# A four-stage graph network kernel: 31 picked passes for 27, last-edge marks through the destination one-hots, one sum per pick, two transfers moved to ScalarE's queue

## What is computed

```
L0:  a_e   = tanh(relu(sum((x[src] @ A1' + b1) * (x[dst] @ A2' + b2 + rel_emb[type])) / sqrt(32)))
     nei   = segment_sum(a_e * sum_b w_comp[type, b] * (x[src] @ weight[b]), dst)
     curr  = x[src of the last edge of each node] @ self_loop_weight
     x     = norm(x + relu(nei + curr))
L1:  x     = norm(x + segment_sum(x[src], dst))
L2:  x     = norm(x + attention over the same edges)
L3:  x     = norm(x + ten propagation steps over the same edges)
```

## Time and profile before

| | us |
|---|---|
| median of 3 runs (lowest, highest) | 1147.88 (1146.41, 1151.34) |
| the profiled execution | 1148.57 |
| its span, first to last instruction | 1146.8 |
| busy: PE, DVE, ACT, POOL | 883.4, 933.5, 504.8, 608.6 |
| mean granted TensorE clock | 0.878 of 2.4 GHz |
| first product of the sweep (L1387) | 70.45 |
| last base columns (L1411) begin | 806.10 |

### The profile page before, as it was taken

How to read it: one execution, slowest core, us unless ns; L and a number is a source line. 1 busy time by engine, 2 the same in 40 slices (tenths; PEclk the granted TensorE clock), 3 DMA queues, 4 the chain that set the end, 5 groups by cost and what they waited for, 6 DMA issues and landing times.

```text
span 1146.8 us, 56069 instructions
## 1 busy us (share of the span) xinstructions
PE 883.4 (77%) x23682; PEld 838.9 (73%) x23682; DVE 933.5 (81%) x2369; ACT 504.8 (44%) x1244; POOL 608.6 (53%) x580
## 2 busy tenths in 40 slices
PE   2358887978686868777867768688468958999996
PEld 2357877877686867776767667587467958999996
DVE  8869999998898989898888988798557995555556
ACT  1135555554454546566756566556567400000000
POOL 5777777777777777777777777774000000000000
PEclk9569999888888888888988897978578979999998
DMA  4432333332232333232323322320000000000001
GB/s 117 60 75 55 64 59 60 66 57 51 48 60 54 57 52 59 52 57 57 57 56 56 51 54 50 68 45 13 5 2 3 4 2 4 5 4 4 4 5 19
DMA packets 54917, 47.97 MB, mean 42 GB/s; under 512 B 35966, under 2 KB 45182, under 8 KB 54662
## 3 DMA queue, kind: packets, MB, share of 16 engines
q0 software_dynamic: 18176, 9.34, 10.3%
q1 hardware_dynamic: 30822, 14.16, 6.1%
q10 hardware_dynamic: 5664, 20.84, 4.9%
HBM read 41.98 MB, written 2.31 MB: 39 GB/s over the span
## 4 chain that ended last, share of the span: by engine, by line
POOL 42%; DVE 19%; PE 18%; issue 16%; DMA 2%; ACT 2%; DVEq 0%; SPq 0%; ACTq 0%
POOL arena L631 42%; PE ps L883 14%; DVE arena L1372 2%; DVE arena L1612 2%; PE ps L854 2%; PE ps L893 2%; DVE arena L1411 2%; DVE arena L1632 1%; ACT arena L1120 1%; DMA arena<-line_table 1%; DMA arena<-rel_rows_in 1%; DVE aggT L1424 1%; DVE arena L1362 1%; PE ps L816 1%; DVE arena L1387 0%
## 5 line engine op out<-in xcount | busy, mean ns | idle before, releaser
L631 POOL DMA_INDIRECT arena<-x_pad,arena x568 | 606.8, 1068 | 173.4 <-issue 172.5
L816 PE MATMUL ps<-aggT 128*128 128x128 f16 x3024 | 217.3, 238 | 1.6 <-DVE aggT L1424 1.3
L816 PEld LDWEIGHTS ps<-aggT 128*128 128x128 f16 x3024 | 205.6, 110 | 3.1 <-DVE aggT L1424 3.1
L1372 DVE TENSOR_SCALAR arena<-pair_no,arena 128x275 bf16<-128x275 f16 (+2 forms) x784 | 183.1, 292 | 0.0
L883 PE MATMUL ps<-arena,adj_words 128*128 128x64 f16 x5625 | 171.9, 192 | 3.4 <-DVEq L1697 3.2
L883 PEld LDWEIGHTS ps<-arena,adj_words 128*128 128x128 fp8e4 x5625 | 170.5, 97 | 4.7 <-DVEq L1697 3.6
L1411 DVE TENSOR_TENSOR arena<-ps,arena 128x1536 f32<-128x1536 f32 x98 | 171.6, 1751 | 0.6
L1073 ACT ACTIVATE adj_words<-arena 128x500 uint8 x196 | 126.5, 646 | 56.5 <-ACT arena L1048 54.2
L1043 ACT ACTIVATE arena<-ps 128x500 fp8e4<-128x500 f32 x196 | 113.0, 577 | 86.9 <-PE ps L765 86.7
L758 PE MATMUL ps<-arena 128*128 128x25 bf16 x195 | 36.5, 187 | 148.7 <-DVE arena L1372 148.3
L778 PE MATMUL ps<-arena 128*32 128x44 f32 (+4 forms) x7048 | 131.3, 212 | 17.6 <-DVE arena L1411 17.5
(11 more groups left out here) (221 smaller groups left out, 1160.6 us busy)
## 6 DMA issues: line engine op xcount, KB each, us to landing
arena<-line_table ACTq DMA_DIRECT2D x48, 344.0 KB
arena<-x_pad,arena POOLq DMA_INDIRECT x568
arena<-pick_table SPq DMA_DIRECT2D x27, 256.0 KB
arena<-line_table ACTq DMA_DIRECT2D x48, 80.0 KB
arena<-dst_parts SPq DMA_DIRECT2D x196, 5.7 KB
agg_table<-arena SPq DMA_DIRECT2D x196, 2.5 KB
dst_parts<-aggT SPq DMA_DIRECT2D x1, 735.0 KB, 12.7
x<-x_pad SPq DMA_DIRECT2D x1, 400.0 KB
```

Of the source, the lines that this page charges most:

```text
L631: pool.indirect_dma_start(to, None, table, bass.IndirectOffsetOnAxis(ap=index, axis=0)).then_inc(done, 16)
L816: mm = nc.tensor.matmul(ps[:, at:at + PICK_WIDE * FEAT], pick_hot[:, u % PICK_RING, k * P:(k + 1) * P], x_parts[:, t, j * PICK_WIDE:(j + 1 ...
L1372: last = v.tensor_scalar(pair_hot[:, d % 2, k, 0:n], pair_no[:, 0:n], pair_of[:, d * DUO + k // SLOTS, k % SLOTS:k % SLOTS + 1], None, ALU ...
```

## The change

- `PICK_UNITS` becomes (3, 2, 2) alone: a duo is picked every three duos (5, 8, 11 to 95), 31 in all.
- The two adds of a pick become one reduction over the four candidates (L1441, L1445), which lie 32 values (128 bytes) apart.
- The one-hots of the destinations are made in pairs: the first of a pair is the last-edge mark, from `off_twice` = (offset + 1) x is-last, the second the destination, from offset + 1. Both are bf16. `weight_e` has pairs too: 1.0 and the weight. The weighting multiplies them and writes both into `mixed`, as its 17th and a new 18th column; the base columns are made from the 18th. The separate marks (L1397) go.
- ScalarE applies a relu after the tanh, with a wait between, since the weighting no longer clips.
- x is loaded by ScalarE's queue under a semaphore of its own, `x_loaded`; the second, larger store of the parts is issued by ScalarE's queue ahead of its first line loads.

```diff
--- before.py
+++ after.py
@@ -72,20 +72,20 @@
...
 PICK_LIMIT = 500.0
-PICK_UNITS = ((2, 2, 2, 1), (3, 2, 2))
+PICK_UNITS = ((3, 2, 2),)
...
     starts, units, picked, at = [], {}, [], 1
-    while at + len(PICK_UNITS[len(picked) % 2]) + 1 < DUOS:
+    while at + len(PICK_UNITS[len(picked) % len(PICK_UNITS)]) + 1 < DUOS:
         c, deep = len(picked), 0
-        for d, n in enumerate(PICK_UNITS[c % 2]):
+        for d, n in enumerate(PICK_UNITS[c % len(PICK_UNITS)]):
...
         starts.append(at)
-        at += len(PICK_UNITS[c % 2])
+        at += len(PICK_UNITS[c % len(PICK_UNITS)])
@@ -242,7 +242,7 @@
...
         hot_no = sb("hot_no", [P, HOTS], BF16)
-        next_no = sb("next_no", [P, HOTS], BF16)
+        next_no = sb("next_no", [P, HOTS, 2], BF16)
@@ -268,12 +268,13 @@
...
-        ARENA = 23880
+        ARENA = 23840
...
         base_t = stay.cut(GROUPS + 1, I32)
-        pair_of, dst_off, last_off_1 = [stay.cut(GROUPS * SLOTS).rearrange("p (g k) -> p g k", k=SLOTS) for _ in range(3)]
+        pair_of = stay.cut(GROUPS * SLOTS).rearrange("p (g k) -> p g k", k=SLOTS)
+        off_twice = stay.cut(2 * GROUPS * SLOTS, BF16).rearrange("p (g k i) -> p g k i", k=SLOTS, i=2)
@@ -293,6 +294,7 @@
...
         dst_t, next_t = [of.bitcast(I32).rearrange("p (g k) -> p g k", k=SLOTS) for of in (dst_words, next_words)]
+        dst_off, last_off_1 = [prep.cut(GROUPS * SLOTS).rearrange("p (g k) -> p g k", k=SLOTS) for _ in range(2)]
@@ -311,13 +313,13 @@
...
         lines = sweep.cut(LINE_BUFS * LINE * WINDOW, BF16, n=SIDE).rearrange("p (h e) -> p h e", h=LINE_BUFS)
-        score, weight_e = [sweep.cut(2 * WIDE).rearrange("p (h k) -> p h k", h=2) for _ in range(2)]
-        dst_hot = sweep.cut(2 * LINE * SLOTS * HOTS, BF16).rearrange("p (h k d) -> p h k d", h=2, d=HOTS)
-        weighted = sweep.cut(WIDE * HOTS).rearrange("p (k d) -> p k d", k=WIDE)
+        score = sweep.cut(2 * WIDE).rearrange("p (h k) -> p h k", h=2)
+        weight_e = sweep.cut(2 * WIDE * 2).rearrange("p (h k i) -> p h k i", h=2, i=2)
+        dst_hot = sweep.cut(2 * LINE * SLOTS * HOTS * 2, BF16).rearrange("p (h k d i) -> p h k d i", h=2, d=HOTS, i=2)
...
         row_hot = sweep.cut(2 * WIDE * P, BF16).rearrange("p (h k v) -> p h k v", h=2, k=WIDE)
-        mixed = sweep.cut(2 * WIDE * HOTS * MIXES).rearrange("p (h k d m) -> p h k d m", h=2, k=WIDE, d=HOTS)
+        mixed = sweep.cut(2 * WIDE * HOTS * (MIXES + 1)).rearrange("p (h k d m) -> p h k d m", h=2, k=WIDE, d=HOTS)
@@ -402,7 +404,7 @@
...
-        inputs_loaded = sem("inputs_loaded")
+        inputs_loaded, x_loaded = sem("inputs_loaded"), sem("x_loaded")
@@ -420,7 +422,7 @@
...
         side_in = [sem(f"side_in_{u}") for u in range(SIDES)]
-        side_made = sem("side_made")
+        tanh_made = sem("tanh_made")
@@ -469,7 +471,7 @@
...
-        LOADS = 14
+        LOADS = 13
@@ -505,7 +507,7 @@
...
                 sp.dma_start(to, of).then_inc(edges_loaded, 16)
-            loads = [(x[:], x_pad.rearrange("(b p) f -> p b f", p=P)), (a12[:, 0:FEAT], a1_t), (a12[:, FEAT:2 * FEAT], a2_t),
+            loads = [(a12[:, 0:FEAT], a1_t), (a12[:, FEAT:2 * FEAT], a2_t),
@@ -530,7 +532,6 @@
...
             sp.dma_start(by_block[:, 0:FIRST_STORED], q_parts[:, 0:FIRST_STORED]).then_inc(first_parts_stored, 16)
-            sp.dma_start(by_block[:, FIRST_STORED:BLOCKS], q_parts[:, FIRST_STORED:BLOCKS]).then_inc(parts_stored, 16)
@@ -702,13 +703,14 @@
...
         def _(pe):
-            pe.wait_ge(inputs_loaded, 16 * LOADS)
+            pe.wait_ge(x_loaded, 16)
...
+            pe.wait_ge(inputs_loaded, 16 * LOADS)
@@ -1013,7 +1015,9 @@
...
+            act.dma_start(x[:], x_pad.rearrange("(b p) f -> p b f", p=P)).then_inc(x_loaded, 16)
             act.wait_ge(inputs_loaded, 16 * LOADS)
+            act.wait_ge(x_loaded, 16)
@@ -1031,6 +1035,9 @@
...
             last.then_inc(rows_made, 1)
+            act.wait_ge(parts_split, 1)
+            act.dma_start(dst_parts.rearrange("(b p) (j c) -> p b j c", p=P, j=3)[:, FIRST_STORED:BLOCKS],
+                          q_parts[:, FIRST_STORED:BLOCKS]).then_inc(parts_stored, 16)
@@ -1090,7 +1097,9 @@
...
                     act.wait_ge(score_ready, d + 1)
-                    a.activation(weight_e[:, d % 2, :], score[:, d % 2, :], ACT.Tanh, scale=1.0 / sqrt(FEAT))                     .then_inc(weight_ready, 1)
+                    a.activation(score[:, d % 2, :], score[:, d % 2, :], ACT.Tanh, scale=1.0 / sqrt(FEAT)).then_inc(tanh_made, 1)
+                    act.wait_ge(tanh_made, d + 1)
+                    a.activation(weight_e[:, d % 2, :, 1], score[:, d % 2, :], ACT.Relu).then_inc(weight_ready, 1)
@@ -1267,7 +1276,7 @@
...
             link(v.tensor_scalar(flag_parts[:, 7:8], base_t[:, GROUPS - 1:GROUPS], float(NODES - PAGE), None, ALU.is_lt))
-            dve.wait_ge(inputs_loaded, 16 * LOADS)
+            dve.wait_ge(x_loaded, 16)
@@ -1287,12 +1296,14 @@
...
                                         op0=ALU.mult, op1=ALU.add))
-            link(v.scalar_tensor_tensor(out=last_off_1, in0=dst_off, scalar=1.0, in1=last_off_1, op0=ALU.add, op1=ALU.mult))
+            link(v.scalar_tensor_tensor(out=off_twice[:, :, :, 0], in0=dst_off, scalar=1.0, in1=last_off_1, op0=ALU.add,
+                                        op1=ALU.mult))
+            link(v.tensor_scalar(off_twice[:, :, :, 1], dst_off, 1.0, None, ALU.add))
...
-            link(v.tensor_scalar(next_no[:], hot_no[:], 1.0, None, ALU.add))
+            link(v.tensor_scalar(next_no[:], hot_no[:].unsqueeze(2).to_broadcast([P, HOTS, 2]), 1.0, None, ALU.add))
@@ -1339,6 +1350,7 @@
...
                 link(v.memset(square_sums, 0.0))
+                link(v.memset(weight_e, 1.0))
@@ -1349,9 +1361,9 @@
...
                 def make_dst_hot(c):
-                    n = [P, LINE * SLOTS, HOTS]
-                    link(v.tensor_tensor(dst_hot[:, c % 2], hot_no[:].unsqueeze(1).to_broadcast(n),
-                                         dst_off[:, c * LINE:(c + 1) * LINE, :].rearrange("p g k -> p (g k)").unsqueeze(2)
+                    n = [P, LINE * SLOTS, HOTS, 2]
+                    link(v.tensor_tensor(dst_hot[:, c % 2], next_no[:].unsqueeze(1).to_broadcast(n),
+                                         off_twice[:, c * LINE:(c + 1) * LINE].rearrange("p g k i -> p (g k) i").unsqueeze(2)
@@ -1390,27 +1402,21 @@
...
-                def make_last(d):
+                def weigh(d):
+                    at = d % LINE_DUOS * WIDE
...
                         dve.wait_ge(mixed_used, d - 1)
-                    n = [P, WIDE, HOTS]
-                    v.tensor_tensor(mixed[:, d % 2, :, :, BASES], next_no[:].unsqueeze(1).to_broadcast(n),
-                                    slots_of(last_off_1, d).rearrange("p g k -> p (g k)").unsqueeze(2).to_broadcast(n),
-                                    ALU.is_equal)
-
-                def weigh(d):
-                    at = d % LINE_DUOS * WIDE
                     dve.wait_ge(weight_ready, d + 1)
-                    step(v.scalar_tensor_tensor(out=weighted,
-                                                in0=weight_e[:, d % 2, :].unsqueeze(2).to_broadcast([P, WIDE, HOTS]), scalar=0.0,
-                                                in1=dst_hot[:, d // LINE_DUOS % 2, at:at + WIDE, :], op0=ALU.max, op1=ALU.mult))
+                    n = [P, WIDE, HOTS, 2]
+                    step(v.tensor_tensor(mixed[:, d % 2, :, :, BASES:BASES + 2], weight_e[:, d % 2].unsqueeze(2).to_broadcast(n),
+                                         dst_hot[:, d // LINE_DUOS % 2, at:at + WIDE], ALU.mult))
...
                                     fetched_of(d)[:, :, SCORED:REL_COLS].unsqueeze(2).to_broadcast(n),
-                                    weighted.unsqueeze(3).to_broadcast(n), ALU.mult).then_inc(mixed_ready, 1)
+                                    mixed[:, d % 2, :, :, MIXES:MIXES + 1].to_broadcast(n), ALU.mult).then_inc(mixed_ready, 1)
@@ -1424,8 +1430,6 @@
...
-                picked_of = picked.rearrange("p (k w f) -> p k w f", k=WIDE, w=PICK_WIDE)
-
@@ -1434,15 +1438,11 @@
...
-                def add_halves():
-                    half = PICK_WIDE // 2
+                def add_picked(c):
...
                     dve.sem_inc(pick_read, 1)
-                    step(v.tensor_tensor(picked_of[:, :, 0:half], picked_of[:, :, 0:half], picked_of[:, :, half:PICK_WIDE], ALU.add))
-
-                def add_pairs(c):
-                    chain.wait()
-                    step(v.tensor_tensor(xp[:, PICKED[c] % AHEAD, :, 0:FEAT], picked_of[:, :, 0, :], picked_of[:, :, 1, :], ALU.add))
+                    step(v.tensor_reduce(xp[:, PICKED[c] % AHEAD, :, 0:FEAT],
+                                         picked.rearrange("p (k w f) -> p k f w", k=WIDE, w=PICK_WIDE), AX.X, ALU.add))
@@ -1463,16 +1463,13 @@
...
                     if picked_now is not None:
-                        add_halves()
+                        add_picked(picked_now)
...
                         make_pairs(d + 1, 6, WIDE)
```

(3 more changed lines are left out.)

## The result

The changed kernel takes 1171.88 us in the median (1170.56 to 1173.11), the kernel before 1148.30 in runs beside it: ratio 1.0203, interval 1.0177 to 1.0228, so 2.0% slower, where 1117.0 was forecast. The profiled execution took 1173.11, its span 1171.2.

The account below looks back on a forecast made before the run. GpSimd's gathers bound the kernel; after the change VectorE would end last. Its terms, -54.9 + 25.7 - 6.9 + 4.5 = -31.6 us, took 1148.57 to 1117.0 us, range 1095 to 1142.

Parts of the forecast that it names:

- GpSimd's line: GpSimd issues gathers without a stop: 534 instead of 568, last issue at 743.4 us, end of sweep -53.7 us.
- The pick count's share: On VectorE: no gather waited for, -54.9 us; a pick with two adds costs 4.88 us, 31 picks for 27.
- The marks and the weighting: On VectorE: marks go from 98 duos, weighting's pace goes from 0.17 to 0.27 us: -6.9 us, bounds -9.8 to +6.9.
- the Relu's price: ScalarE's relu after tanh, 0.3 us with its wait, charged only the 15 times L1404 already waits: +4.5 us.
- The setup: Loads before the sweep: x load +1.5 to +3 us beside edge loads; line load 0, bounds -3 and +4.
- The price of the sum: VectorE's single sum of 1024 elements at the mask's pace, 1.14 us: 0.20 dearer per pick; all picks +25.7 us.
- rival 1: The strided sum on VectorE pays 0.81 us more a pick, 25 us in all: 1142 us; chance 0.17.
- VectorE's line: VectorE's paces from start to start: terms sum to -31.6 us, 22 us later than GpSimd's, so it sets the end.
- the term "nothing" for TensorE: 28 more units of 16 matmuls cost nothing: TensorE is busy 42 of 50 us where VectorE is full.
- Rival 3: ScalarE's queue falls behind at one duo in three, 31 more waits of 0.3 to 0.5 us: 1127 to 1133; chance 0.16.
- Rival 4: TensorE at low clock becomes the bound; mean sweep clock of 0.87 or less makes it slower than before (1154); chance 0.05.
- The slower side: Chance 0.06 that the change is slower: TensorE at low clock 0.05, a table load at every tanh-relu turn 0.01.

Follow-up runs that it names:

- b_picks31: Kernel before with 31 picked passes in place of 27, nothing else: 1118.21 us, ratio 0.9729.
- a_adds: Changed kernel with the two adds of each pick in place of the one strided sum: 1122.41 us, ratio 0.9753.
- b_queues: Kernel before with only the x load and the second store of the parts on ScalarE's queue: 1150.40 us, ratio 0.9995.
- a_sum_behind: Changed kernel with the one sum behind the last two pair one-hots of the next duo, not ahead of them: 1141.74 us, ratio 0.9933.
- a_noclip: Changed kernel without the Relu on ScalarE, so negative weights are not clipped: 1166.10 us, ratio 1.0147.
- the dense filler: Unread 840-element reduction added to the changed kernel with two adds: 1141.48 us behind the pair one-hots, 1167.42 ahead, 1131.57 in the next duo.
- b_onesum: Kernel before with the two adds of a pick done as one strided reduction, nothing else: 1141.87 us, ratio 0.9928.
- b_best2: Kernel before with 31 picked passes, compares spread 2, 3, 2, and ScalarE's copy of moved sums behind the counts' copies: 1098.24 us, ratio 0.9558.

## Why the prediction was wrong

The time of 1117.0 and the range up to 1142 both missed; the sign too. By its terms the forecast had -35.4 us for the passes with two adds, -2.4 for the marks, the weighting, the Relu and the setup, and +6.2 for the sum (31 x 0.20). The runs gave -31.6, +4.2 and +49.5, together +22.1 where the change itself measured +23.6. The first two miss by 10 us together, the sum by 43.

- **GpSimd's line** was right in kind: 534 gathers, no product waits for them. Its last issue came at 760 and not 743, with 30.6 us of waits for buffers that came free late. It isn't that alone: in b_picks31, with 0.6 us of such waits, it came at 761.41, as each gather took 1102 ns and not 1068.
- **The pick count's share** was right. By the prediction's own terms 31 passes with two adds are -54.9 + 4 x 4.88 = -35.4 us; b_picks31 measured -31.6 (1149.8 to 1118.2). That the forecast for the whole change was -31.6 too is chance.
- **The marks and the weighting**: 0.35 us as forecast, and the destination one-hots stayed at 0.33. With the Relu and the queues they cost 4.2 us (a_adds less b_picks31, from two groups of runs, so not clear of noise), where -6.9 + 4.5 was put down.
- **The reading behind the Relu's price**, "VectorE is 2 to 4 us from tanh's result in most duos", was wrong. In the trace of the kernel before, the weighting starts 2 us or more behind the end of tanh in 28 of 98 duos, and less than 0.5 behind it in 39. So ScalarE had little to spare in many duos already, and the term that rests on it was too sure; in the changed kernel the weighting waits for ScalarE 41 times where it waited 15.
- **The setup**: +3.4 us, inside the bounds of -3 and +4; the edge loads did pay for the x load beside them (1.5 us, as by bytes), and the line load was 1.4 longer. Alone (b_queues) the first product is as late, at 73.59, and the time is within the noise of no change.
- **The price of the sum** is the first step that failed: "I take the mask's pace, 1.14". It is 1.79 from start to start, 1866 ns, so L1264 was the row that it is like and L1637 was not. (1866 - 155) / 1024 = 1.67 ns an element. (The 155 is only what L1637 leaves at 1.1 ns an element; by L1484, 196 in a row in 348 ns, the rest is 132, and then L1637 too paid 0.3 ns more an element than a row does.) The Trainium skill (SBUF — State Buffer, Door 1: The DMA port swizzle) has the rule that every access to another 16-byte line pays; the trace agrees for this sum, and the prediction should have given the rule, not its one short exception, the price. That was rival 1, and it would have given 1142, still faster. The 1141.7 of a_sum_behind is close to it in part by luck: the length cost 19.3 and not 25 there, and the other parts cost more than forecast.
- **The place of the sum** is the second, and the larger: the sum of terms charged each operation its length on VectorE's line, as if that line could only be delayed by its own work. But the term "nothing" for TensorE and the term of 1.14 for the sum left out that TensorE's counts wait for the pair one-hots behind the sum, and that ScalarE's tanh stands behind the copy that waits for TensorE. 31 passes x 0.97 us = 30.1 us came that way (a_sum_behind), and the sum's length cost 19.3 of the 29 by which it is longer. The old order had split the sum in two around these pair one-hots; the diff shows it, and I priced the second add's move at nothing.
- **Rival 3** named the symptom, ScalarE late more often, with 10 to 16 us against 41.6 of added wait; the wait passed the 30 us that the prediction had set as its sign. It put the lateness down to ScalarE's own queue, and not to what that queue waits for. Without the Relu (a_noclip) the wait is 47.1 us for 56.8, and the time 5.8 less, so it is a part and not the source. The counting pieces weren't tried apart, but the traces bound them: at 73 to 330 us, where none runs, the weighting waits 10.7 us in the changed kernel and 0.5 in the one before, and at 580 to 835, with one in nearly every duo, 27.8 and 11.4. So the wait grows with the pieces in both kernels, and an excess of 10 is there without them.
- **Rival 4**, TensorE at low clock, asked for 0.87 or less in the sweep, and the sweep has 0.86. But it is not shown as the cause: both timelines have a slow run of counts behind the rest, and TensorE is busy only 3.4 us longer in the changed kernel than with the sum behind. TensorE's rests are what the moves changed. That some part of the 30.1 goes through the clock stays open.
- **The slower side** got 0.06. The sum took VectorE as the one full engine and the others as free, while TensorE was 78 to 82% busy in the windows above and fed ScalarE, and ScalarE VectorE, in one ring per duo, of which the sum of terms had no entry.

## What to carry to other kernels

When a change takes the last slack out of an engine that several others take turns with, price each operation by its place as well: list which semaphores are raised behind it, and by whom they are awaited. Here a reduction of 1.03 us cost 1.45 us a time ahead of a signal (45.0 / 31) and 0.62 behind it (19.1 / 31). And test parts singly *in the changed kernel* too: on the kernel before, whose slack paid for everything, each part looked harmless.

## What the runs showed of the hardware

- One strided reduction, 1024 fp32 values read 128 bytes apart, costs 1866 ns (1906 in a_sum_behind), where the dense filler takes 1028 for 840. Two adds over the same 1024 values have paces of 0.94 in sum.
- The gather on GpSimd takes 1048 ns beside the reduction and 1068 beside the two adds, all else the same (b_onesum). The Trainium skill (SBUF — State Buffer, Who interferes with whom) says that a VectorE instruction with two inputs in SBUF contends with GpSimd's reads and a reduction never does; these two numbers go that way, by 2%. But it moves by more for other reasons: 1102 ns at 31 passes with two adds, and 1066 with the same instructions in b_best2, where only the order of compares and of one copy differs. What sets it was not settled.
- Behind a rest of 3.65 us, and behind one of 1.93, TensorE's eight counts took 1.03 and 0.96 us, and 0.63 a duo later. The granted clock is 0.50 at 616.1 to 617.1 us of the changed kernel and 1.00 at 624.8 to 625.4; with the sum behind it is 1.00 during the rest (593.4 to 595.2) and 0.56 at 595.3 to 596.3. So here even the short rest is followed by the low level.
